# Turning chunks by VectorE blocks and a trip through DRAM in place of identity matmuls

## The chip, the cores and the metric

One core of a Trainium2 chip runs the whole kernel. The metric is the device time of one execution in microseconds (us); the median of the kernel before is 1278.88 us over three runs (1278.22 to 1279.74).

## What is computed

`x` is (8, 2048, 64) in fp32, `adj` a (2048, 2048) matrix A whose rows are a 0/1 pattern divided by the row's sum. Four layers, each `x = layernorm(x + f(x))` over the last 64:

```
layer 0:  out = sum over k of (T_k x) w_k[n] + b[n]    T_0 = I, T_1 = A, T_2 = 2 A A - I
          w_k[n] = sum over d < 16 of embedding[n, d] * weight[d, k]   (its own 64x64 per node n)
layer 1:  twice: z = relu((A z) W)
layer 2:  out = x Ws + (A x) Wn + bias
layer 3:  x1 = A x;  x2 = 2 A x1 - x;  out = [x, x1, x2, x1, x2] Wcat + bias
```

## The kernel before

**Layout.** The eight batches are four pairs, j = 0 to 3; a pair's 2 x 64 features are 128 columns. A pair's state lies in `nat` as [128 nodes, 16 node tiles x 128 features], and is handled in four chunks c of 512 columns. The 0/1 pattern of A stays in SBUF as `B` (128 x 16 x 2048, fp32r); the row factors are `rrep`.

**A pass.** One multiplication with A for one pair is a pass p. `split` (L743 on ScalarE, L874 on VectorE) writes the state as a high and a low fp32r part into `xs`. `mm` (L659, `pe_quarter` L605) multiplies: a chunk c of the result takes four quarters m of 8 matmuls of 128x512 each, 32 in all, into one PSUM bank. The state is the stationary operand, so the product comes out turned: features on partitions, nodes along the row. `scale` (L862) multiplies it by `rrep` into one slot per lane, `y = ring[:, 4 + n]` (n = j % 2), or for the first passes of pairs 0 and 1 into a slot of its own each.

Passes by number: 0 and 1 belong to layer 0, 2 and 3 to layer 1, 4 to layer 2, 5 and 6 to layer 3. After the product of chunk c comes `after`:
- p = 0: the scaled product is turned back to nodes on partitions by four identity matmuls (`pe_turned`, L618 to L621, called at L674), ScalarE copies it from PSUM into `nat` (L759); it is the source of pass 1. SyncE stores y itself into `y1d` (L1070) for later.
- p = 2, 3: y is weighed, `pe_weighed` (L623): four matmuls (each stands as two records in the profile) with y as stationary operand, which turns it on the way.
- p = 4, 5: the input of the chunk is needed too, turned. The step `ahead` does that with four identity matmuls on `nat` (L679) and a ScalarE copy into the lane's single slot `ring[:, n]` (L784); the weighing (L692) takes that slot and y, 8 matmuls, 16 records. For p = 5 y is also turned (L674) and copied into `stg` (L780), as source of pass 6.
- p = 6: y weighed, the last addition, the output.
Passes 3, 4 and 6 end in a layernorm: `centre`, `deviate`, `normed` (L902 to L922 on VectorE, L785 to L795 on ScalarE). GpSimd adds the biases (L1000).

**Order.** `order()` (L38) writes one list of steps by hand, and every engine runs its part of the list in order; semaphores tie them together. Each queue blocks on the first wait in it. `head()` loads A in tiles and runs pass 0 of pairs 0 and 1 as the tiles come; `second_pass0()` (L188) runs pass 1 of pair 0 while pair 1's pass-0 products are turned, then SyncE loads layer 0's weights (`weights0`, L1063). Then four stages, one per pair, run the per-node products of layer 0 (`T`, L717, each 10 matmuls of 128x512, with 8 VectorE accumulations at L974 per step) woven with quarters of the passes of the next pair (`weave`, L209). From `put("W")` (L284) on come two lanes: lane 0 is pair 2 and then pair 0, lane 1 pair 3 and then pair 1. They take turns; a lane's turn is one chunk, or one of the two `yield`s that stand before each pass and have no matmul of their own (the last chunk's `after` falls to the next turn as well). So now and then a lane runs two or three chunks with nothing of the other's between them.

**In a chunk of passes 4 and 5** the list reads: quarter 0 of chunk c, then `finish(c - 1)` (its `after`, and in pass 4 `deviate` of c-2, `centre` of c-1, `normed` of c-2), quarters 1 to 3, `ahead` of c, `scale` of c.

SyncE issues every DMA of the kernel in the order of the list. PSUM banks are handed out at L441 to L479; `xT_after` (L511) says when the slot `ring[:, n]` is free: when the weighing of the chunk before it is done.

Of the kernel before, what the change touches and what calls it, by code (L numbers as in the profile page):

```python
# [36 lines left out]

def order():  # L38
# [5 lines left out]
    def one_pass(j, p):  # L44

        norm = p in (3, 4, 6)

        def finish(c):
# [12 lines left out]
        for c, m in order:  # L61
            put("mm", j, p, c, m)
            if c > 0 and p >= 2 and m == (3 if c == 1 and order[2] == (1, 0) else 0):
                finish(c - 1)
            if m < 3:
                yield False
                continue
            if c > 0 and p < 2:
# [242 lines left out]
def gnn_stack(nc, xn, xt, at, rb, r16, emb, embt, b0, w01, w2, wbd, bias, eye, eps, out, zd, y1d, bd):  # L311
# [3 lines left out]
    with ctx:  # L315
# [47 lines left out]
        def way(general):  # L363
# [14 lines left out]
            s_wl = sem("wload")  # L378
# [3 lines left out]
            s_turn, s_turny, s_four, s_T = sem("turn"), sem("turny"), sem("four"), sem("T")  # L382
# [4 lines left out]
            s_lo, s_y, s_v = sem("lo"), sem("y"), sem("v")  # L387
            s_mean, s_var, s_norm, s_Lo, s_Sl = sem("mean"), sem("var"), sem("norm"), sem("Lo"), sem("Sl")
            s_acc, s_w0, s_twl, s_W = sem("acc"), sem("w0"), sem("twl"), sem("W")
            s_sum1, s_sum2, s_rec, s_Wc = sem("sum1"), sem("sum2"), sem("rec"), sem("Wc")  # L390
# [5 lines left out]
            else:  # L396
                s_at = [[sem(f"at{m}{c}") for c in range(PIECES.get(m, 1))] for m in range(NT)]
# [4 lines left out]

            def ahead(j, p, c):
                return Step("ahead", j, p, c)

            def after(j, p, c):
# [9 lines left out]
            turn_at = numbered("ahead")  # L416
            turny_at = {s: i + 1 for i, s in enumerate(s for s in STEPS if s.kind == "after" and s.p in (0, 5))}
            four_at = {s: i + 1 for i, s in enumerate(s for s in STEPS if s.kind == "after" and s.p > 1)}
            evict_at = {s: i + 1 for i, s in enumerate(
                s for s in STEPS if s.kind == "ahead" or s.kind == "after" and s.p in (0, 2, 5))}  # L420
# [18 lines left out]


# [4 lines left out]
            turn, held = [0, 1], {b: (s_evict, evict_at[after(1, 0, b)]) for b in range(2)}  # L445
# [14 lines left out]
            turn, held = [2, 3], {b: (s_evict, evict_at[after(1, 0, b)]) for b in (2, 3)}  # L460
# [7 lines left out]
            for i, s in enumerate(STEPS):  # L468
                if i == SECOND:
                    turn = turn + [6, 7]  # L470
                if s.kind == "after" and s.p == 0 and s.j < 2:
                    nbank_of[s, "turn"] = bank_of["prod", s.j, 0, s.c]
                    nbank_after[s, "turn"] = None
                elif s.kind == "ahead" or s.kind == "after" and s.p in (0, 5):
# [10 lines left out]
            held = [[(s_y1o[1], 64), (s_turny, turny_at[after(1, 0, c)])] for c in range(2)]  # L485
            for s in STEPS:
# [4 lines left out]
                elif s.kind == "scale" and s.p != 1:  # L491
                    y_after[s] = held[n]
                    if s.p == 0:
                        n_y1o[n] += 16
                        y1o_at[s.j, s.c] = n_y1o[n]
                        held[n] = [(s_y1o[n], n_y1o[n]), (s_turny, turny_at[after(s.j, 0, s.c)])]
                    else:
                        held[n] = [(s_four, four_at[after(s.j, s.p, s.c)])]
                if s.kind == "loadx":
# [14 lines left out]
            for s in STEPS:  # L514
                n = s.j % 2
                if s.kind == "ahead":
                    xT_after[s] = held_x[n]
                    held_x[n] = (s_four, four_at[after(s.j, s.p, s.c)])
                if s.kind == "centre" and s.p > 1:
                    if (s.j, s.p) == (2, 3):  # L520
                        sq_after[s] = (s_var, var_at[Step("deviate", 2, 3, s.c - 1)]) if s.c else None
                    else:
                        sq_after[s] = held_q[n]
                        held_q[n] = (s_var, var_at[Step("deviate", s.j, s.p, s.c)])

# [50 lines left out]

            def xs_free(j, p, c):
# [7 lines left out]
            def source_of(j, p, c):  # L585
# [8 lines left out]
                if p == 1:  # L594
                    return ch(nat[n], c), s_evict, evict_at[after(j, 0, c)]
# [4 lines left out]
                if p == 6:  # L600
                    return ch(stg[n], c), s_evict, evict_at[after(j, 5, c)]
# [28 lines left out]
            def pe_steps(pe, steps):  # L630
                for s in steps:
# [38 lines left out]
                    if s.kind == "after" and p in (0, 5):  # L670
# [4 lines left out]
                    if s.kind == "ahead":  # L675
                        pe.wait_ge(s_norm, norm_at[Step("normed", j, p - 1, c)])
                        if nbank_after[s, "turn"]:
                            pe.wait_ge(*nbank_after[s, "turn"])
                        pe_turned(pe, nbank_of[s, "turn"], ch(nat[n], c)).then_inc(s_turn, 1)  # L679
                    if s.kind == "after" and p > 1:  # L680
# [48 lines left out]
            def act_steps(ac, steps):  # L729
                for s in steps:  # L730
# [5 lines left out]
                    if s.kind == "tile" and not general:  # L736
                        cols = piece(k, c)
                        ac.wait_ge(s_at[k][c], 16)
# [4 lines left out]
                    if s.kind == "split":  # L743
                        src, landed, v = source_of(j, p, c)
                        ac.wait_ge(landed, v)
# [6 lines left out]
                    if s.kind == "after" and p == 0:  # L752
# [20 lines left out]
                    if s.kind == "after" and p == 5:  # L773
                        ac.wait_ge(s_turny, turny_at[s])
                        if j == 2:
                            ac.wait_ge(s_T, n_T)
                        else:
                            ac.wait_ge(s_hi, split_at[Step("split", j, 3, c)])
                            ac.wait_ge(s_lo, split_at[Step("split", j, 3, c)])
                        ac.copy(ch(stg[n], c), ps[:, nbank_of[s, "turn"], :]).then_inc(s_evict, 1)  # L780
                    if s.kind == "ahead":
                        ac.wait_ge(s_turn, turn_at[s])
                        ac.wait_ge(*xT_after[s])
                        ac.copy(ring[:, n, :], ps[:, nbank_of[s, "turn"], :]).then_inc(s_evict, 1)  # L784
# [52 lines left out]
            def dve_steps(dv, steps):  # L837
                for s in steps:
# [35 lines left out]
                    if s.kind == "split":  # L874
                        src, landed, value = source_of(j, p, c)
# [359 lines left out]
```

## Time and profile before

| | |
|---|---|
| median of 3 runs | 1278.88 us (1278.22 to 1279.74) |
| the profiled execution's own time | 1277.89 us |
| its span | 1276.1 us |
| TensorE matmul / weight load | 1249.3 us (98%) / 1046.2 us (82%) |
| VectorE | 730.8 us (57%) |
| ScalarE | 241.2 us (19%) |
| GpSimd | 62.2 us (5%) |
| DMA packets, bytes | 28517, 55.08 MB |

The profile's durations of single matmuls overlap (they are pipelined), so what one costs is read from the distance of the starts or from the chain of waits, which cuts the span into pieces that do not overlap. The chain covers the span from the last instruction backwards.

### The profile page before, as it was taken

How to read it: one execution, taken by the hardware profiler on the slowest of the kernel's cores; microseconds unless marked ns; L12 is line 12 of the kernel's file. 1: busy time of each engine (PE TensorE's matmuls, PEld its weight loads, DVE VectorE, ACT ScalarE, POOL GpSimd, SP SyncE). 2: the span in 40 equal slices, each digit the busy share in tenths (PEclk: the TensorE clock that was granted, in tenths of full speed). 3: DMA queues.
4: the chain of work that ended last, by engine and by line, in shares of the span. 5: the costliest groups of instructions: out<-in, count | busy, mean ns of one | idle time of the engine just before them, and what ended most of it. 6: DMA issues, size and time to landing. Idle time of an engine off the chain costs nothing.

```text
span 1276.1 us, 16492 instructions
## 1 busy us (share of the span) xinstructions
PE 1249.3 (98%) x6048; PEld 1046.2 (82%) x6048; DVE 730.8 (57%) x1819; ACT 241.2 (19%) x436; POOL 62.2 (5%) x52
## 2 busy tenths in 40 slices
PE   8999999999999999999999999999999999999996
PEld 6888888788878887878888888888888888888875
DVE  5836888786777777787624533551256245335424
ACT  5622111121112011110202121120202021211110
POOL 0000000000000000000001011000000010010000
PEclk9999999999999999999999999999999999999998
DMA  9732122221211111120000000010001000000000
GB/s 338 322 99 59 38 58 54 71 54 38 54 47 57 38 38 38 30 62 1 15 1 1 1 1 1 4 64 1 1 25 42 1 1 1 1 1 1 34 1 36
DMA packets 28517, 55.08 MB, mean 43 GB/s; under 512 B 3584, under 2 KB 14336, under 8 KB 26368
## 3 DMA queue, kind: packets, MB, share of 16 engines
q1 hardware_dynamic: 28432, 53.96, 12.9%
q8 instruction: 52, 0.85, 0.3%
q14 instruction: 33, 0.27, 0.1%
HBM read 41.89 MB, written 12.06 MB: 42 GB/s over the span
## 4 chain that ended last, share of the span: by engine, by line
PE 91%; DVE 5%; DMA 1%; issue 1%; ACT 1%; SPq 1%; DVEq 0%; ACTq 0%
PE ps L608 29%; PE ps L609 29%; PE ps L717 20%; PE ps L626 8%; PE ps L620 2%; PE ps L647 2%; PE ps L648 2%; DVE nat L974 1%; DVE ring L974 1%; DMA raw<-in_at 1%; DVE xs L884 1%; ACT xs L751 0%; SPq L1014 0%; DVE sml L916 0%; DVE sml L907 0%
## 5 line engine op out<-in xcount | busy, mean ns | idle before, releaser
L608 PE MATMUL ps<-B,xs 128*128 128x512 f32 x1664 | 658.1, 395 | 4.2 <-DVE xs L884 4.2
L609 PE MATMUL ps<-B,xs 128*128 128x512 f32 x1664 | 649.0, 390 | 0.0
L608 PEld LDWEIGHTS ps<-B,xs 128*128 128x128 f32 x1664 | 312.7, 188 | 67.8 <-ACT xs L751 3.9
L609 PEld LDWEIGHTS ps<-B,xs 128*128 128x128 f32 x1664 | 313.0, 188 | 61.7
L717 PE MATMUL ps<-Tw,xs 128*128 128x512 f32 x1280 | 309.4, 391 | 2.5 <-DVE ring L974 2.5
L717 PEld LDWEIGHTS ps<-Tw,xs 128*128 128x128 f32 x1280 | 238.6, 188 | 55.1 <-DVE ring L974 4.8
L872 DVE TENSOR_TENSOR ring<-ps,rrep 128x512 f32<-128x512 f32 x94 | 64.4, 689 | 277.6 <-PE ps L609 269.4
L974 DVE SCALAR_TENSOR_TENSOR nat<-ps,embn,nat 128x128 f32<-128x128 f32 x448 | 153.4, 342 | 51.0 <-PE ps L717 50.8
L974 DVE SCALAR_TENSOR_TENSOR ring<-ps,embn,ring 128x128 f32<-128x128 f32 x512 | 174.8, 341 | 0.0
L626 PEld LDWEIGHTS ps<-W,ring 128*128 128x128 f32 x896 | 110.4, 191 | 7.9 <-DVE ring L872 3.6
L626 PE MATMUL ps<-W,ring 128*128 128x128 f32 x896 | 113.2, 275 | 2.3 <-DVE ring L872 2.3
L789 ACT ACTIVATE ring<-nat 128x512 f32<-128x512 f32 x60 | 37.9, 632 | 313.2 <-DVE nat L911 313.2
L901 DVE TENSOR_TENSOR nat<-ps,nat 128x512 f32<-128x512 f32 x48 | 33.1, 690 | 66.7 <-PE ps L626 66.7
L1000 POOL TENSOR_TENSOR nat<-nat,bias 128x512 f32<-128x512 f32 x32 | 41.4, 1293 | 578.7 <-PE ps L620 578.7
L884 DVE TENSOR_TENSOR xs<-nat,xs 128x512 fp32r<-128x512 f32 x72 | 45.7, 685 | 21.3 <-ACT xs L751 20.9
L794 ACT ACTIVATE sml<-sml,epst 128x8 f32<-128x8 f32 x64 | 19.3, 301 | 186.8 <-DVE sml L916 186.8
L647 PE MATMUL ps<-B,xs 128*128 128x512 f32 x128 | 52.1, 407 | 2.4 <-DVE B L846 2.4
L784 ACT COPY ring<-ps 128x512 f32<-128x512 f32 x32 | 18.8, 587 | 177.6 <-PE ps L620 177.6
L648 PE MATMUL ps<-B,xs 128*128 128x512 f32 x128 | 51.4, 401 | 0.0
L993 POOL TENSOR_TENSOR nat<-nat,ring 128x512 f32<-128x512 f32 x16 | 20.6, 1289 | 586.9 <-DVE ring L974 586.9
L974 DVE SCALAR_TENSOR_TENSOR nat<-ps,embn,ring 128x128 f32<-128x128 f32 x64 | 22.3, 348 | 46.8 <-PE ps L717 46.0
L819 ACT CAST xs<-ring_x 128x512 fp32r<-128x512 f32 x32 | 19.6, 619 | 149.8 <-PE ps L717 116.7
(65 smaller groups left out, 625.9 us busy)
## 6 DMA issues: line engine op xcount, KB each, us to landing
raw<-in_at SPq DMA_DIRECT2D x13, 1024.0 KB, 17.0
ring<-in_xn SPq DMA_DIRECT2D x16, 256.0 KB, 2.9
ring_x<-in_xt SPq DMA_DIRECT2D x32, 128.0 KB, 3.3
ring_x<-y1d SPq DMA_DIRECT2D x32, 128.0 KB, 3.4
out<-nat SPq DMA_DIRECT2D x16, 256.0 KB, 2.4
y1d<-ring SPq DMA_DIRECT2D x14, 256.0 KB, 2.7
zd<-nat SPq DMA_DIRECT2D x12, 256.0 KB, 2.9
nat<-zd SPq DMA_DIRECT2D x3, 1024.0 KB, 4.9
```

Source lines behind the costliest of these rows:

```text
L608: pe.matmul(bank, x[:, 0, m, :], of, start=m == 0, stop=False)
L609: mm = pe.matmul(bank, x[:, 1, m, :], of, start=False, stop=ends and m == NT - 1)
L626: mm = pe.matmul(ps[:, bank, k * P:(k + 1) * P], src[:, k * P:(k + 1) * P], w, start=i == 0, stop=i == len(pairs) - 1)
L647: pe.matmul(bank, xs[n][:, 0, k, :], of, start=k == 0, stop=False)
L648: mm = pe.matmul(bank, xs[n][:, 1, k, :], of, start=False, stop=k == LAST)
L717: mm = pe.matmul(ps[:, 4 + 2 * p + q, :], src, Tw[:, wi, 512 * p:512 * p + 512], start=i == 0, stop=i == 4)
L789: ac.activation(square_slot(j, p, c), ch(nat[n], c), ACT.Square).then_inc(s_sq, 1)
L872: dv.tensor_tensor(to, ps[:, bank_of["prod", j, p, c], :], ch(rrep, 0 if general else c), ALU.mult).then_inc(s_y, 1)
L884: dv.tensor_tensor(lo, src, hi.bitcast(F32), ALU.subtract).then_inc(s_lo, 1)
L901: dv.tensor_tensor(v, bank, v, ALU.add).then_inc(s_v, 1)
L974: dv.scalar_tensor_tensor(sums[d % 2], ps[:, 4 + 2 * p:6 + 2 * p, i * C:(i + 1) * C], embn[:, t, d:d + 1], first[d] if d < 2 else sums[d % 2],
L1000: po.tensor_tensor(g, g, bias_t[:, p - 4, :].unsqueeze(1).to_broadcast([P, 8, C]), ALU.add).then_inc(s_pb, 1)
```

## The change

The four identity matmuls of a chunk and ScalarE's copy are replaced, for all chunks except those named by `on_pe`, by: VectorE transposes the 32x32 blocks of the chunk in place of the tile (`dv.transpose`, 128x512), SyncE stores the result (256 KB) into a DRAM scratch `td`, waits for it, and issues four loads of 64 KB, one for each group of 32 destination partitions, that bring the blocks to the place of the transposed chunk; each load reads runs of 32 elements (128 bytes). `ahead` is gone; its place is `turn` with k = 0, whose slot is still `ring[:, n]`. `turn` with k = 1 turns y into `nat` (p = 0) or `stg` (p = 5). In pass 0 `finish(c - 1)` moves up, from the end of chunk c to its quarter 1 (for c = 1 it stays at quarter 3). Six of the loads of A (tiles 9 to 14) share the semaphore of the tile seven earlier, and SyncE waits until ScalarE has read that tile. Some semaphores are merged. The store and the loads stand in SyncE's queue at the place of the step.

```diff
+def on_pe(j, p, c):
+    return p == 0 and (j == 0 or j > 1 and c == 3) or (j, p, c) == (1, 5, 3)
...
         def finish(c):
             put("after", j, p, c)
+            if p == 0 and not on_pe(j, p, c):
+                turn(c, 1)
...
         for c, m in order:
+            if p in (4, 5) and (c, m) == (0, 0):
+                turn(0, 0)
             put("mm", j, p, c, m)
+            if c > 0 and p == 0 and m == (3 if c == 1 else 1):
+                finish(c - 1)
             if c > 0 and p >= 2 and m == (3 if c == 1 and order[2] == (1, 0) else 0):
                 finish(c - 1)
+                if p in (4, 5):
+                    turn(c, 0)
...
-            if p in (4, 5):
-                put("ahead", j, p, c)
             put("scale", j, p, c)
+            if p == 5 and not on_pe(j, p, c):
+                turn(c, 1)
...
             if 2 <= i < 6:
                 put("after", 1, 0, i - 2)
+                put("turn", 1, 0, i - 2, 1)
+                put("back", 1, 0, i - 2, 1)
...
-                if s.kind == "ahead":
+                if s.kind == "turn" and s.k == 0:
                     xT_after[s] = held_x[n]
                     held_x[n] = (s_four, four_at[after(s.j, s.p, s.c)])
...
+            def turn_source(j, p, c, k):
+                return y_slot(j, p, c) if k else ch(nat[j % 2], c)
+
+            def turn_slot(j, p, c, k):
+                if k == 0:
+                    return ring[:, j % 2, :]
+                return ch(nat[j % 2] if p == 0 else stg[j % 2], c)
...
                         if p in (4, 5):
                             pe.wait_ge(s_W, 1)
-                            pe.wait_ge(s_evict, evict_at[ahead(j, p, c)])
+                            pe.wait_ge(*landed(j, p, c, 0))
...
+                    if s.kind == "turn":
+                        if k == 0:
+                            dv.wait_ge(s_norm, norm_at[Step("normed", j, p - 1, c)])
+                            dv.wait_ge(*xT_after[s])
+                        else:
+                            dv.wait_ge(s_y, scale_at[Step("scale", j, p, c)])
...
+                        dv.transpose(turn_slot(j, p, c, k), turn_source(j, p, c, k)).then_inc(s_turn, 1)
...
+                    if not s_at[m]:
+                        sp.wait_ge(s_nz, tile_at[Step("tile", 0, 0, 0, m - 7)])
...
+                    if s.kind == "turn":
+                        sp.wait_ge(s_turn, turn_at[s])
+                        sp.dma_start(td[n, k, c], turn_slot(j, p, c, k)).then_inc(s_away, 16)
+                    if s.kind == "back":
+                        v = moved_at[s._replace(kind="turn")]
+                        sp.wait_ge(s_away, 16 * turn_at[s._replace(kind="turn")])
+                        if v > 1:
+                            sp.wait_ge(s_back[n][k], 64 * (v - 1))
+
+                        blocks = td[n, k, c].rearrange("(a i) (t b m) -> b i t a m", i=32, t=4, m=32)
+                        for b in range(4):
+                            to = turn_slot(j, p, c, k)[32 * b:32 * b + 32, :].rearrange("i (t a m) -> i t a m", t=4, m=32)
+                            sp.dma_start(to, blocks[b]).then_inc(s_back[n][k], 16)
```

The helper `turn(c, k)` of `one_pass` puts the steps `turn` and `back` one after the other; `landed(j, p, c, k)` is the count of `s_back` at which a chunk's four loads have landed.

## Rows read from the trace of the kernel before

**Rows 1.** The page: busy time by engine, and the chain that ended last.
```profile
PE 1249.3 (98%) x6048; PEld 1046.2 (82%) x6048; DVE 730.8 (57%) x1819; ACT 241.2 (19%) x436; POOL 62.2 (5%) x52
...
PE 91%; DVE 5%; DMA 1%; issue 1%; ACT 1%; SPq 1%; DVEq 0%; ACTq 0%
```
**Rows 2.** Groups by shape, TensorE: count, busy us, mean ns, idle before.
```profile
L620 PE MATMUL ps<-identf,nat 128*128 128x128 f32 x128 | 19.1, 272 | 0.0
```
**Rows 3.** The chain in 1195 to 1235 us: start, us, what.
```profile
1198.29 0.23 PE ps L609
1198.53 0.44 PE ps L620 x4
```
**Rows 4.** The chain from 655 us: weighings of passes 4 and 5, pair 2.
```profile
664.02 1.78 PE ps L626 x16
...
674.44 1.78 PE ps L626 x16
...
683.98 1.78 PE ps L626 x16
...
698.96 1.78 PE ps L626 x16
...
735.23 1.79 PE ps L626 x16
...
746.12 1.79 PE ps L626 x16
...
756.13 1.79 PE ps L626 x16
```
**Rows 5.** DMA issues by line: count, KB each, median us from issue to landing.
```profile
y1d<-ring SPq DMA_DIRECT2D x14, 256.0 KB, 2.7
...
ring_x<-y1d SPq DMA_DIRECT2D x32, 128.0 KB, 3.4
...
ring<-in_w SPq DMA_DIRECT2D x2, 512.0 KB, 4.8
```
**Rows 6.** SyncE's queue in order of time: start, us, line, what.
```profile
81.48 4.65 SPq L1070 DMA_DIRECT2D y1d<-ring_x  x2
86.25 0.36 SPq L1066 DMA_DIRECT2D ring<-in_w  x1
...
110.62 0.61 SPq L1087 DMA_DIRECT2D ring_x<-in_xt  x1
111.28 0.60 SPq L1088 DMA_DIRECT2D ring_x<-y1d  x1
```
**Rows 7.** DMA in 153:155.05, 110.5:115, 79.6:81.35: packets, MB, share of 16 engines.
```profile
q1 hardware_dynamic: 144, 0.26, 33.1%
...
q1 hardware_dynamic: 288, 0.26, 20.1%
...
q1 hardware_dynamic: 144, 0.00, 4.4%
```
**Rows 8.** VectorE behind two weighings of pass 4, in order of time.
```profile
667.50 0.69 DVE L911 TENSOR_TENSOR nat<-nat,sml 128x512 f32<-128x512 f32 x1
...
679.22 0.69 DVE L921 TENSOR_TENSOR nat<-nat,sml 128x512 f32<-128x512 f32 x1
```
**Rows 9.** VectorE in 85 to 125 us, in order of time.
```profile
94.18 1.20 DVE L925 TENSOR_TENSOR ring<-ring 64x1024 f32<-64x1024 f32 x1
...
100.52 1.89 DVE L884 TENSOR_TENSOR xs<-nat,xs 128x512 fp32r<-128x512 f32 x3
...
107.71 0.69 DVE L872 TENSOR_TENSOR nat<-ps,rrep 128x512 f32<-128x512 f32 x1 [4.10 <-PE ps L609]
```
**Rows 10.** TensorE at the start, and stretch 12 to 13 us (busy, then clock).
```profile
14.05 0.63 PE L648 MATMUL ps<-B,xs 128*128 128x512 f32 x1
14.47 0.63 PE L647 MATMUL ps<-B,xs 128*128 128x512 f32 x1
...
12.00:13.00 1.00, 1.00 (x4) 0.81 (x3) 0.33 (x3) 0.67 (x2) 0.00 (x0) 1.00 1.01 365
```

More of the change, by code:

```diff
@@ L396, in way @@
             else:
-                s_at = [[sem(f"at{m}{c}") for c in range(PIECES.get(m, 1))] for m in range(NT)]
+                s_at = [[sem(f"at{m}{c}") for c in range(PIECES.get(m, 1))] if m < 9 or m == LAST else None
+                        for m in range(NT)]
                 s_r = [sem(f"r{c}") for c in range(NC)]
@@ L438, in way, with turned, landed @@
                     held[i] = s
+            def turned(j, p, c):
+                if on_pe(j, p, c):
+                    return s_turny, turny_at[after(j, p, c)]
+                return s_turn, turn_at[Step("turn", j, p, c, 1)]
+            def landed(j, p, c, k):
+                return s_back[j % 2][k], 64 * moved_at[Step("turn", j, p, c, k)]
             bank_of = {("prod", j, 0, c): 4 - 4 * j + c for j in range(2) for c in range(NC)}
             bank_after = {}
-            turn, held = [0, 1], {b: (s_evict, evict_at[after(1, 0, b)]) for b in range(2)}
+            turn, held = [0, 1], {b: (s_y, scale_at[Step("scale", 1, 0, b)]) for b in range(2)}
             for i, s in enumerate(STEPS):
@@ L459, in way @@
             nbank_of, nbank_after = {}, {}
-            turn, held = [2, 3], {b: (s_evict, evict_at[after(1, 0, b)]) for b in (2, 3)}
+            turn, held = [2, 3], {b: (s_y, scale_at[Step("scale", 1, 0, b)]) for b in (2, 3)}
             def take(use, frees):
@@ L484, in way @@
             y1o_at = {}
-            held = [[(s_y1o[1], 64), (s_turny, turny_at[after(1, 0, c)])] for c in range(2)]
+            held = [[(s_y1o[1], 64), turned(1, 0, c)] for c in range(2)]
             for s in STEPS:
@@ L594, in source_of @@
                 if p == 1:
-                    return ch(nat[n], c), s_evict, evict_at[after(j, 0, c)]
+                    return ch(nat[n], c), *((s_evict, evict_at[after(j, 0, c)]) if on_pe(j, 0, c) else landed(j, 0, c, 1))
                 if p == 2 and j < 2:
@@ L669, in pe_steps @@
                             mm.then_inc(s_prod, 1)
-                    if s.kind == "after" and p in (0, 5):
+                    if s.kind == "after" and on_pe(j, p, c):
                         pe.wait_ge(s_y, scale_at[Step("scale", j, p, c)])
@@ L751, in act_steps @@
                             ac.copy(part_of(j, 0, c), src).then_inc(s_hi, 1)
-                    if s.kind == "after" and p == 0:
+                    if s.kind == "after" and p == 0 and on_pe(j, p, c):
                         ac.wait_ge(s_turny, turny_at[s])
@@ L772, in act_steps @@
                         ac.copy(ch(to, c), ps[:, nbank_of[s, "four"], :]).then_inc(s_evict, 1)
-                    if s.kind == "after" and p == 5:
+                    if s.kind == "after" and p == 5 and on_pe(j, p, c):
                         ac.wait_ge(s_turny, turny_at[s])
[L775 to L779, printed above, removed]
+                        ac.wait_ge(s_hi, split_at[Step("split", j, 3, c)])
+                        ac.wait_ge(s_lo, split_at[Step("split", j, 3, c)])
                         ac.copy(ch(stg[n], c), ps[:, nbank_of[s, "turn"], :]).then_inc(s_evict, 1)
[L781 to L784, printed above, removed]
                     if s.kind == "centre":
```

82 lines of the change are left out of this document (47 added, 35 removed).

## The prediction

> **What bounds the kernel now.** I read the page first. TensorE is busy in 98% of the span and holds 91% of the chain that ended last [rows 1], so whatever leaves its queue comes off the time, and whatever makes it wait goes on it. Next the turns by identity matmul: 256 of them, four to a chunk of 128x512, 64 chunks; the largest of their three groups is [rows 2], the others have 120 and 8. The mean of one, 272 ns, is not its price: the chain of waits gives four of them 0.44 us between their neighbours, as it gives 0.23 us to one product matmul [rows 3]. Then I read the end stage, from 613 us, where two pairs of batches ("lanes") take turns by chunk. The 16-matmul pieces of the chain are the weighings of passes 4 and 5, 32 chunks. Their starts show how long TensorE has other work between one weighing and the next of the same lane: 15 us when the other lane has a chunk there, but 9.5 to 10.9 us when it has none [rows 4]. Last, VectorE's rows behind a weighing, the DMA rows, and the stretch from 80 to 113 us.
>
> **Part 1: what leaves TensorE.** By `on_pe`, 4 chunks of pair 0 and the last chunks of pairs 2 and 3 in pass 0, and one of pass 5, stay: 7. The 57 others go: 32 "ahead", 15 of pass 5, 10 of pass 0. 57 x 0.44 = 25.1 us off the path [rows 3]. The Trainium skill ("TensorE: Matmul & The Clock Gate", section "Part 4: PE-mode transpose") gives some 275 ns for one turn inside a kernel; by that 228 of them would be 63 us and the sum below would end near 1273. The trace agrees with 275 as a duration (272), not as a price, so that end gets no chance of its own.
>
> **Part 2: what VectorE and ScalarE get.** 57 transposes of 128x512. No such row exists; the nearest, one 128x512 operation, takes 0.69 [rows 9], and I take that; bounds 0.35 (twice as fast) and 1.3. That is 39 us on an engine that is busy 57%. ScalarE loses 57 evictions, which were off the path and are worth nothing. The added load matters only through the waits of part 4.
>
> **Part 3: the new way of a chunk (R).** Transpose, store to DRAM, wait for its landing on SyncE's queue, four loads. The store: 2.7 us to landing as y1d's (2.3 to 2.9 over all stores of this size) [rows 5]. Each load is 64 KB in 512 runs of 128 bytes. Issues of loads with rearranged patterns start 0.66 apart [rows 6] and land in 3.4 [rows 5]; the fourth lands 3 x 0.66 + 3.4 = 5.4 after the first is issued. Do the short runs take longer than that? From the share of 16 engines, windows of 2.05, 4.5 and 1.75 us: 2 KB runs 84 ns, 1 KB runs 56 ns, 4-byte runs 8.6 ns each [rows 7]. A line through the first two gives 31 ns at 128 bytes, one through the last two 14; an engine has 128 runs in the four loads, so 1.8 to 4.0 us, inside the 5.4. I take 5.5. R = 0.69 + 2.7 + 5.5 + 0.3 for the hand-overs = 9.2 us. Low end: 0.35 + 2.3 + 0.2 + (3 x 0.45 + 2.9) = 7.1. High end: runs that cost what 1 KB does, 128 x 0.056 = 7.2, plus 1.8 of issue and confirmation = 9.0 for the loads, R = 12.6 to 13.
>
> **Part 4: who waits (47 of the 57 are in the end stage).** The turned input lies in one slot per lane (`ring[:, n]`). So the turn of chunk c waits for the weighing of c-1 (`xT_after`), and TensorE, in order, waits at the weighing of c (`landed`). Between the two it has the distance of their starts [rows 4], less the weighing (1.78) and the turns that are gone (0.44 in pass 4, 0.88 in pass 5): 10.42 gives 8.2 and 9.54 gives 7.3 in pass 4; 10.89 gives 8.2 and 10.01 gives 7.3 in pass 5. Against that stands VectorE's work queued ahead of the turn, plus R. In pass 4 the centring of c-1 comes first: for c = 1 from the group's end at 665.80 to 668.19, 2.4 us; for c = 2 to the end of the norm at 679.91 after a group that ended at 676.22, 3.7 us [rows 4, 8]. In pass 5 only the addition, 0.75. So:
> - Pass 4, c = 1: 2.4 + 9.2 = 11.6, against 8.2 twice and 7.3 twice: 2 x 3.4 + 2 x 4.3 = 15.4.
> - Pass 4, c = 2: 12.9 against 7.3, twice (pairs 2 and 0): 11.2.
> - Pass 5: 9.95 against 8.2 twice, 7.3 five times: 3.5 + 13.3; and the last chunk of pair 1, where only 24 matmuls (5.45) stand between: 4.5. Together 21.3.
> That is 14 waits, 47.9 us. Elsewhere the cover is 10.4 us or more (12.8 for c = 3 of pass 4, against 12.9) and I cost it at nothing; it goes if R is over 10. The products of pass 5 (k = 1) have 16 to 60 us until their splits; their loads hold SyncE's queue some 5.5 us, which hits the next turn by 1.7 at most, and then the wait before it has already moved it: nothing.
>
> **Part 5: the head of the kernel.** Pair 1's four turns stand in SyncE's queue ahead of `weights0`. Each holds it for a y1d store's issue, the landing and four issues: 0.45 + 2.7 + 0.1 + 2.6 = 5.85 us. From about 82 us, near the y1d stores that start at 81.48, the weights would be asked for at 104.7 instead of 86.25 and land 4.8 later, at 109.6 [rows 5, 6]; VectorE's work on them starts there instead of at 94.18, a shift of 15.4 [rows 9]. Behind it in VectorE's queue stand pair 1's splits (now at 100.52) that TensorE wants at 107.5, when pair 0's pass ends and its last scaling starts [rows 9]. Slack of about 6.3, minus a handful of tenths for the hand-over: TensorE waits 9.3 us. With 4.7 a turn the shift is 11 and the wait 4.7. In passes 0 of pairs 2 and 3 the turn has about 10 us until its split; 1 us for both together, as SyncE's queue also holds the fetches. The raw loads that now wait for the tile seven earlier are costed at nothing: the six loads between are still in flight then and hide it; without them the head would wait for each load's landing.
>
> **Sum.** 47.9 + 9.3 + 1 - 25.1 = +33. The profiled execution took 1277.9 (1.0 under the median of 1278.88, a difference I ignore): 1311.
>
> **The rivals.**
> - *All lands in time (faster).* R under 6.4 us hides every wait but the head's: 1277.9 - 25.1 + 4.7 = 1257. For it: landings of 2.3 and 2.9 exist. Against: those two alone with three more issues and the transpose are 7.1. 8%.
> - *Break-even.* All at the low end, R = 7.1: pass 4 2 x 1.3 + 2 x 2.2 + 2 x 3.5 = 14.0, pass 5 5.2, head 4.7, minus 25.1: 1277. 13%, a third of it on either side of the 0.2%.
> - *The waits also cost clock.* In the first microseconds product matmuls start 0.42 to 0.43 apart, about what the lower of the two levels (1.2 GHz) would make of the 0.23 later, though the granted clock is given as 1.00 there [rows 3, 10]. If each of the eight waits over 3.4 us cost a stretch like the 14 matmuls that go at this pace, 14 x 0.2 = 2.8 us, that is 22 more: 1333. Against it: nothing shows what a wait of 4 us does here. 11%.
> - *Short runs are slow.* At R = 12.6: pass 4 47 for c = 1 and 2 and 13 for the rest, pass 5 48, head 23, weave 1, minus 25: 1385. The Trainium skill ("DMA: Bandwidth & Descriptors", section "Rules for kernel authors") says to turn data by the DMA's own transpose and not by a plain copy with a rearranged pattern, which it puts at 19 times slower. By it this rival would be the likely one. Here VectorE does the fine part, and the small runs of [rows 7] show no such price. 10%.
>
> **How the numbers follow.** My forecast, 58%, spans 1285 to 1345 for R from 7.8 to 10.2. The range 1270 to 1350 leaves out the full gain and the slow runs. Under 0.2% (2.6 us, about what a measurement can tell) 5%; faster 12%; slower 83%.
>
> **What would show it.** Identity matmuls x28; TensorE waits at L626's successor put down to the DMA that reads `td`, 13 or 14 of them, 2 to 6 us each, in pairs; loads landing 3.4 after issue; VectorE busy near 770; the weights asked for near 105 and the first per-node product near 122 instead of 113. It is wrong if a weighing follows its predecessor by 9.1 us with no wait, or if waits appear where the cover is 15 us.

## The result, and the profile after

The changed kernel takes 1340.12 us (median of 4 runs, 1338.52 to 1345.48); the kernel before took 1278.55 beside it (1277.48 to 1279.74). The ratio is 1.0489 with a 95% interval of 1.0457 to 1.0520: slower by 61.6 us, where the prediction said slower by 33, range 1270 to 1350. The profiled execution took 1338.52 (span 1336.7, mean granted clock 0.975, before 0.996).

The page of the changed kernel: busy time by engine, DMA packets, and the chain that ended last, by engine.

```profile
PE 1247.7 (93%) x5820; PEld 1039.0 (78%) x5820; DVE 766.3 (57%) x1876; ACT 209.0 (16%) x379; POOL 62.3 (5%) x52
...
DMA packets 157111, 84.99 MB, mean 64 GB/s; under 512 B 124880, under 2 KB 135632, under 8 KB 154960
...
PE 68%; DVE 11%; DMA 11%; SPq 6%; issue 3%; ACT 1%; DVEq 0%; ACTq 0%
```

Beside [rows 1]: TensorE runs 228 matmuls fewer and holds 68% of the chain instead of 91%. What came in is DMA (11%) and SyncE's queue (6%), the trip that a turned chunk now makes. The chain shows how often that trip was the last thing missing.

The page, DMA issues by line (count, KB each, median us from issue to landing):

```profile
td<-ring SPq DMA_DIRECT2D x32, 256.0 KB, 2.0
ring<-td SPq DMA_DIRECT2D x128, 64.0 KB, 2.5
```

The store of a turned input lands in 2.0 (that of a product of pass 5 in 2.4) and a load in runs of 128 bytes in 2.5, against 2.7 for y1d's store and 3.4 for y1d's loads [rows 5]. Who waits, on TensorE (us in total, times, longest):

```profile
PE ps L671 <- DMA ring<-td: 40.5, 15, 4.9
PE ps L653 <- DVE xs L917: 19.2, 6, 12.8
PE ps L665 <- DVE ring L905: 6.4, 3, 3.0
```

L671 is the weighing (L626 before), L653 the product (L608 before), L665 the identity matmul that stayed. 15 weighings wait for the loads of their turned input; one product waits 12.8 us, in the head.

**Where the 60.6 us of the two profiled spans lie.** The per-node products T cut the kernel into three. First and last start of the 1280 of them, by source line, before and after:

```profile
L717 PE MATMUL ps<-Tw,xs x1280: 387/389/502, 112.9 to 604.0; 128*128 128x512 f32 x183
```

```profile
L757 PE MATMUL ps<-Tw,xs x1280: 387/389/628, 126.7 to 624.3; 128*128 128x512 f32 x183
```

The head got longer by 13.8 us, the woven middle by 6.5 (491.1 to 497.6), the end stage by 40.3 (672.1 to 712.4). To each, add the turns that it lost, at 0.44 [rows 3]: 4, 6 and 47 chunks, 1.8, 2.6 and 20.7 us. So the new costs are 15.6, 9.1 and 61.0, the gain is 25.1, and the rest is +60.6.

**One trip in the end stage**, pair 2, pass 4. SyncE's queue, VectorE's and TensorE's in 688 to 712 us (start, us, what, idle before and its releaser):

```profile
689.30 0.33 SPq L1123 DMA_DIRECT2D td<-ring  x1
691.28 2.60 SPq L1133 DMA_DIRECT2D ring<-td  x4
702.34 0.33 SPq L1123 DMA_DIRECT2D td<-ring  x1
704.48 2.78 SPq L1133 DMA_DIRECT2D ring<-td  x4
```

```profile
688.57 0.70 DVE L932 STREAM_TRANSPOSE ring<-nat 128x512 f32<-128x512 f32 x1
...
701.61 0.70 DVE L932 STREAM_TRANSPOSE ring<-nat 128x512 f32<-128x512 f32 x1
```

```profile
695.98 2.02 PE L671 MATMUL ps<-W,ring 128*128 128x128 f32 x16 [1.54 <-DMA ring<-td]
709.36 3.06 PE L671 MATMUL ps<-W,ring 128*128 128x128 f32 x16 [4.05 <-DMA ring<-td]
```

From the start of the transpose to the weighing: 7.4 us and 7.75 us. That is R, forecast at 9.2. Although R is shorter, the second weighing waits 4.05; and it then takes 3.06 us where the first took 2.02. The clock says why (stretch, TensorE busy, granted clock, DMA share, GB/s):

```profile
709.00:710.00 1.00, 0.64 (x6) 1.00 0.00 0
710.00:711.00 1.00, 1.00 (x8) 0.56 0.00 0
711.00:713.00 2.00, 2.00 (x9) 0.50 0.00 0
713.00:714.00 1.00, 1.00 (x5) 0.73 0.00 0
714.00:716.00 2.00, 2.00 (x10) 1.00 0.00 0
```

The clock is still at its upper level (2.4 GHz) for the first part of a microsecond after the wait, then at the lower (1.2 GHz), and back at 714. Work lost: 0.44 + 2 x 0.50 + 0.27 = 1.7 us, paid after the wait ended and put down to no wait at all.

Such a spell of lower clock follows eight of the fifteen waits for turned inputs, each costing 1.7 us, the last (1286 to 1294) 3.4. It is not the length of a wait alone that decides. In the same form, from the ends of waits of 4.41, 2.26, 3.74 and 3.06 us on:

```profile
894.00:899.00 5.00, 4.92 (x23) 0.66 0.28 48
1187.00:1192.00 5.00, 4.75 (x22) 0.66 0.00 0
1080.60:1086.00 5.40, 5.39 (x32) 1.00 0.00 0
1175.60:1181.00 5.40, 5.33 (x32) 1.00 0.00 0
```

Read in stretches of 1 us, TensorE's busy time times the missing share of the clock adds up to 14.5 us in the end stage, 5.1 in the middle (three spells) and 3.5 in the head (two spells). In the kernel before it is nothing in all three.

### The profile page after: what moved, and what is told of

Its sections match the earlier page's. It is cut to its first block, busy times and chain, and to the rows that moved or that the text cites. A ratio compares the mean times of both kernels' runs of the same rounds, so it can differ in the third digit from the quotient of the medians.

```text
span 1336.7 us, 16321 instructions
## 1 busy us (share of the span) xinstructions
PE 1247.7 (93%) x5820; PEld 1039.0 (78%) x5820; DVE 766.3 (57%) x1876; ACT 209.0 (16%) x379; POOL 62.3 (5%) x52
## 4 chain that ended last, share of the span: by engine, by line
PE 68%; DVE 11%; DMA 11%; SPq 6%; issue 3%; ACT 1%; DVEq 0%; ACTq 0%
PE ps L653 21%; PE ps L654 21%; PE ps L757 16%; PE ps L671 7%; SPq L1133 5%; DMA td<-ring 3%; DMA ring<-td 3%; PE ps L692 2%; PE ps L693 2%; DVE nat L1022 2%; DVE ring L1022 2%; DMA td<-nat 1%; DMA ring_x<-y1d 1%; DVE sml L955 1%; DVE ring L905 1%
## 5 line engine op out<-in xcount | busy, mean ns | idle before, releaser
L653 PE MATMUL ps<-B,xs 128*128 128x512 f32 x1664 | 660.3, 397 | 19.2 <-DVE xs L917 19.2
L653 PEld LDWEIGHTS ps<-B,xs 128*128 128x128 f32 x1664 | 316.2, 190 | 85.3 <-issue 17.6
L757 PEld LDWEIGHTS ps<-Tw,xs 128*128 128x128 f32 x1280 | 242.0, 190 | 54.9 <-DVE ring L1022 4.7
L671 PE MATMUL ps<-W,ring 128*128 128x128 f32 x896 | 123.4, 290 | 43.5 <-DMA ring<-td 40.5
L671 PEld LDWEIGHTS ps<-W,ring 128*128 128x128 f32 x896 | 118.6, 203 | 56.5 <-issue 47.7
L791 ACT CAST xs<-nat 128x512 fp32r<-128x512 f32 x72 | 39.7, 615 | 37.7 <-DMA nat<-zd 24.6
## 6 DMA issues: line engine op xcount, KB each, us to landing
raw<-in_at SPq DMA_DIRECT2D x13, 1024.0 KB, 16.7
```

What stands on the lines that cost most here:

```text
L653: pe.matmul(bank, x[:, 0, m, :], of, start=m == 0, stop=False)
L671: mm = pe.matmul(ps[:, bank, k * P:(k + 1) * P], src[:, k * P:(k + 1) * P], w, start=i == 0, stop=i == len(pairs) - 1)
L757: mm = pe.matmul(ps[:, 4 + 2 * p + q, :], src, Tw[:, wi, 512 * p:512 * p + 512], start=i == 0, stop=i == 4)
L791: ac.copy(part_of(j, 0, c), src).then_inc(s_hi, 1)
```

## The experiments

My theory after the result, called A: the loss is the sum of single causes, each at its place: the waits for turned inputs in the end stage, the clock that they cost, and SyncE's queue in the head and the middle. The rivals differ by experiment. All kernels are edits of the changed one (1340.12) unless said otherwise. The kernel before took 1277.9 to 1278.4 us beside each group.

**1. The 32 inputs back on TensorE.** The step `ahead` returns as before; the 15 products of pass 5 and pass 0 stay on the new way.

```diff
-            if p in (4, 5) and (c, m) == (0, 0):
-                turn(0, 0)
...
-                if p in (4, 5):
-                    turn(c, 0)
...
+            if p in (4, 5):
+                put("ahead", j, p, c)
             put("scale", j, p, c)
...
```

> The turned input of passes 4 and 5 (32 chunks) goes back to four identity matmuls and a ScalarE copy; the 15 products of pass 5 and the 10 of pass 0 keep the new way. Theory A (the end stage loses 61 us by the wait for the single slot per lane and by the lower clock after the longest of these waits): those 61 us go and the 32 x 0.44 = 14 us gained come back, 1340 - 61 + 14 = 1293. Theory B (the new transfers and VectorE's transposes slow everything in proportion to their number): 32/57 of the 61.6 us go, 1305.

Measured: 1296.47 (1292.07 to 1297.60), ratio 1.0132 (1.0108 to 1.0156). Its end stage takes 670.7 us (623.4 to 1294.1). Less the 15 turns that are still gone there (6.6), the stage of the kernel before would be 665.5, so 5.2 us of the 61.0 are left. With the inputs' trips gone, 55.8 of them are gone; the products' trips of pass 5 alone cost next to nothing.

**2. Pass 0 back on TensorE** (pairs 1, 2 and 3, 10 chunks), **and 3. pair 1's four alone.**

```diff
-    return p == 0 and (j == 0 or j > 1 and c == 3) or (j, p, c) == (1, 5, 3)
+    return p == 0 and (j == 0 or j in (1, 2, 3) or j > 1 and c == 3) or (j, p, c) == (1, 5, 3)
```

For pair 1 alone the inner list is `(1,)`; with all three, `finish(c - 1)` of pass 0 stands at the end of chunk c again.

> The 10 chunks of pass 0 (pair 1's four, three each of pairs 2 and 3) go back to TensorE, with the order of before there; passes 4 and 5 keep the new way. Theory A (SyncE's queue is held by store, landing and loads, so that layer 0's weights come 20 us late and the fetches of the per-node stages late too: 15.5 us at the head and 9.2 in the stages after, by the distance of marks in the two traces): 1340 - 24.7 + 4.4 = 1320. Theory B (in proportion to the number): 10/57 of 61.6 us, 1329.

> Edit: only pair 1's four pass-0 chunks are turned by TensorE again (head of the kernel); pairs 2 and 3 keep the new way. Theory A (the head loses by the place of the weights behind the four turns in SyncE's queue, and no later slack takes that up): the first per-node product starts again near 113 instead of 126.7, and the time falls by that 13.8 us: 1326. Of the 22 us that came back with all ten pass-0 chunks on TensorE, some 8 would then belong to pairs 2 and 3. Theory B (part of the head's loss is absorbed later, since the passes woven into the per-node products wait for their fetches anyway): less than half of it, 1333 to 1336, and most of the 22 us would be pairs 2 and 3.

Measured: 1317.81 (1311.06 to 1319.91), ratio 1.0288 (1.0259 to 1.0318), and 1328.30 (1326.04 to 1331.16), ratio 1.0399 (1.0383 to 1.0415). Pair 1's four chunks are worth 11.8 us, the six of pairs 2 and 3 another 10.5 by the medians, 6.4 by the middle stages of the two profiles (499.0 and 492.6). With all ten back the first T starts at 112.2 and 40.0 us of waits for turned inputs are left: the head and the end stage do not touch each other. Both times lie nearest to theory A.

**4. Filled waits.** Before 14 weighings TensorE multiplies something that is overwritten afterwards. The counts in the edit add up to 115 matmuls of 128x512, and the trace shows 115; the 121 and 27.5 us of the expectation are a wrong sum (115 x 0.23 = 26.5).

```diff
+                            for _ in range(FILL.get((j, p, c), 0) if not general else 0):
+                                pe.matmul(ps[:, bank, :], B[:, 0, 0:P], B[:, 0, 0:512], start=True, stop=True)
                             pe.wait_ge(*landed(j, p, c, 0))
...
```

> Nothing is undone: ahead of the weighings that waited for the four loads, TensorE gets 5 to 12 extra matmuls of 128x512 into the bank that the weighing overwrites, each 0.23 us, fewer than fit into the wait that the trace shows there (14 places, 121 matmuls, 27.5 us in all), so that it is not idle for over 2 us. Theory A (part of the loss is the clock, which is granted at 0.50 for 3.4 us after a long wait, some 9 times in the end stage at 1.7 us each): 1340 - 12 to 15, 1327. If the clock costs nothing: 1340, or up to 5 us more where a filler is longer than its wait.

Measured: 1328.04 (1324.33 to 1333.37), ratio 1.0384 (1.0348 to 1.0420): 12 us faster by doing more work (8.1 by the spans of the two profiled executions). Its end stage, from the last T at 623.4 to 1328.6, takes 705.2 us against 712.4. Its weighings that wait:

```profile
PE ps L673 <- DMA ring<-td: 16.7, 10, 3.7
```

All waits of the stage fell from 47.2 (40.5 + 6.7 others) to 21.4 (16.7 + 4.7 others). With the fillers that is 21.4 + 26.5 = 47.9 us, no less than the 47.2 that they stand in for, and the stage is 7.2 shorter all the same: 7.9 us to explain. The granted clock explains 6.6 of them: the loss counted as above is 7.9 us where the changed kernel has 14.5, and the spells left follow the three longest waits that are left (3.1 to 3.7 us). The fill was not complete. Three of the 14 places (24 matmuls) had no wait in the changed kernel, and three of its waits (4.41, 4.30 and 3.06) got no filler.

**5. Two slots per lane for the turned input**, the turn issued one chunk earlier.

```diff
             if p in (4, 5) and (c, m) == (0, 0):
                 turn(0, 0)
+                turn(1, 0)
...
-                if p in (4, 5):
-                    turn(c, 0)
+                if p in (4, 5) and c < 3:
+                    turn(c + 1, 0)
...
+                if k == 0 and c % 2:
+                    return W[:, 5:9, :].rearrange("p a b -> p (a b)") if j % 2 else part_slot(0)
...
```

> The turned input gets a second slot per lane (the old ring_g for one lane, the free end of a longer W for the other), and each chunk is turned one chunk earlier, so that 15 us of TensorE's work lie between its transpose and its weighing. The number of transposes, stores and loads is the same. Theory A (the chain through the single slot costs 40.5 us of waits and the clock about 15): 1340 - 55 = 1285, no wait of L671's successor for the loads from td. Theory B (the transfers as such): 1335 to 1340. Between them: if SyncE's queue, which both lanes share, becomes the bound, half the waits stay, 1312.

Measured: 1305.40 (1304.42 to 1306.03), ratio 1.0208 (1.0191 to 1.0225): 34.7 us faster, but 20 short of A's 1285. TensorE's waits in its end stage:

```profile
PE ps L657 <- DVE xs L921: 14.2, 2, 12.8
PE ps L675 <- DMA ring<-td: 7.4, 4, 3.3
```

The single slot was the cause of the waits for turned inputs: 40.5 became 7.4 + 1.7. In their place one of 12.8 us appeared. The chain in 838 to 886 us shows what it is (start, us, what):

```profile
854.88 2.15 DMA td<-ring
...
859.69 2.61 DMA td<-W
...
864.97 2.65 DMA td<-stg
...
870.88 0.62 SPq L1189
...
873.00 3.29 DMA td<-ring
...
878.97 2.56 DMA td<-stg
...
884.32 5.18 DMA nat<-zd
```

The reload of pair 0's state stands behind five trips and the outputs (L1189) in SyncE's queue, each trip a landing and four issues.

**6. Layer 0's weights asked for first**, ahead of pair 1's turns.

```diff
                 put("after", 1, 0, i - 2)
+                if i == 2:
+                    put("wload")
                 put("turn", 1, 0, i - 2, 1)
...
-                    if s.kind == "weights0":
+                    if s.kind == "wload":
```

> Only the place of two DMA issues changes in SyncE's list: layer 0's weights are asked for ahead of pair 1's four turns instead of behind them. Theory A (at the head TensorE waits for what stands in VectorE's queue behind these weights, 12.8 us, and the clock falls with it): 1340 - 13 to 15 = 1326, the first per-node product near 112 us instead of 126.7. Rival (pair 1's turned products themselves come too late, since the four turns still hold SyncE's queue to 107 us): the wait moves to them, 1335 to 1340.

Measured: 1330.61 (1328.94 to 1331.89), ratio 1.0407 (1.0390 to 1.0425), between the two. The first T starts at 114.6 instead of 126.7, but part of it comes back in the middle: the last T starts at 618.2 instead of 624.3, so 6.1 of the 12.1 are left at that point. The trace shows where the other 6.0 went: in the middle the identity matmuls wait 8.4 us instead of 5.6, and the clock costs 8.6 instead of 5.1. By the medians 9.5 us came back of the head's 11.8 (experiment 3).

**7. Two slots and pass 0 on TensorE**, and **8. that with the outputs of pairs 2, 3, 0 and the two late reloads issued by ScalarE's queue**; **9. two slots and the moved outputs, pass 0 as in the change.**

```diff
-                    if s.kind == "reload":
+                    if s.kind == "reload" and j == 2:
...
-                    if s.kind == "out":
+                    if s.kind == "out" and j == 1:
...
+                    if s.kind == "reload" and j != 2:
+                        for i in range(NC):
+                            ac.wait_ge(s_z[n][i], 16)
+                        ac.wait_ge(s_out[n], 64)
+                        ac.dma_start(nat[n][:], zd[j]).then_inc(s_re[n], 16)
+                    if s.kind == "out" and j != 1:
+                        ac.wait_ge(s_norm, norm_at[Step("normed", j, 6, c)])
+                        ac.dma_start(out[j, :, cols], ch(nat[n], c)).then_inc(s_out[n], 16)
```

> Both of the earlier edits together: the second slot per lane, and pass 0 back on TensorE. If the losses are separate, 1305.4 - 22.3 = 1283. If they hide each other (the end stage only starts earlier and waits for the same thing), above 1290; the wait of 12.8 us for pair 0's splits stays in either case.

> As the one before, and the outputs of pairs 2, 3 and 0 and the reloads of pairs 0 and 1 are issued from ScalarE's queue, no longer from SyncE's. Theory A (the 12.8 us wait with two slots is pair 0's reload, asked for at 884 us behind four turns in SyncE's queue, and the clock that falls with it): 1283 - 13 to 17 = 1268, faster than the kernel before by 10. Rival (the reload itself, or the traffic, takes that long): 1283.

> Two slots per lane and outputs and reloads from ScalarE's queue, pass 0 as in the change. Theory A: 1305.4 - 15 = 1290; what is left over the kernel before is then the head and the per-node stages (24.7 less their gain of 4.4). Rival as in the run before: 1305.

Measured, in this order: 1285.93 (1281.76 to 1289.16), ratio 1.0066 (1.0043 to 1.0089); **1271.37 (1268.80 to 1274.06), ratio 0.9950 (0.9935 to 0.9966)**; 1294.01 (1290.64 to 1298.18), ratio 1.0134 (1.0106 to 1.0162). The reload's wait, 13.0 us in the first of them, is gone in the second. The second beats the kernel before by 0.5%. Its waits for turned inputs on TensorE:

```profile
PE ps L671 <- DMA ring<-td: 6.6, 3, 3.6
...
PE ps L671 <- DMA W<-td: 1.7, 1, 1.7
```

Its end stage takes 664.6 us (603.3 to 1267.9): 672.1 of before, less 20.7 of turns, plus 9.0 more of waits than before (12.4 against 3.4), makes 660.4. The remaining 4.2 have a place in the granted clock: three spells, which cost 4.9 us while TensorE was busy. So the price of 0.44 for a turn holds within a microsecond over 47 turns.

**10. A control on the kernel before**: only the moved outputs and reloads.

> A control, made on the kernel before: the outputs of pairs 2, 3 and 0 and the two late reloads are issued by ScalarE's queue instead of SyncE's, as in the version of the changed kernel that came out 0.5% faster than the kernel before. If that gain comes from the turns that left TensorE: no change here, 1278 (1276 to 1280), since TensorE waits in the kernel before for nothing that stands behind an output in SyncE's queue. Rival: the moved outputs would have made any version faster, 1270 or less, and the turns would not be what gained.

Measured: 1277.69 (11 runs, 1277.18 to 1279.97) against 1278.10 (15 runs), ratio 0.9998 (0.9989 to 1.0007). The moved outputs give nothing where no turns crowd SyncE's queue, so the gain of experiment 8 over the kernel before comes with the turns that left TensorE.

**11. The store made twice, one landing after the other.**

```diff
                         sp.dma_start(td[n, k, c], turn_slot(j, p, c, k)).then_inc(s_away, 16)
+                        sp.wait_ge(s_away, 32 * turn_at[s] - 16)
+                        sp.dma_start(td[n, k, c], turn_slot(j, p, c, k)).then_inc(s_away, 16)
...
```

> Edit: SyncE stores each turned chunk twice, one after the other, and waits for the landing in between, so that the way of a chunk is longer by one landing (2.0 us in the profile of the changed kernel) and 0.3 us. Nothing else changes. Theory A (the waits at the weighings are cover minus this way): 13 waits of the end stage grow by 2.3 each, 30 us; the third chunks of pass 4, just covered until now, begin to wait, 4 us; the head gets four times 2.3, 9 us; the weave 4; and longer waits take a further 5 to 10 us of clock. 1340 + 30 + 4 + 9 + 4 + 8 = 1395. Theory B (the waits are set by something that the way of the chunk only shares, such as VectorE's place in the order): less than half of it, under 1365.

Measured: 1426.60 (1421.74 to 1432.32), ratio 1.1161 (1.1130 to 1.1192), 86.5 us more than the change, and above both theories. Its waits:

```profile
PE ps L671 <- DMA ring<-td: 85.5, 20, 9.1
PE ps L653 <- DVE xs L917: 30.0, 6, 21.8
```

The head's wait grew by 9.0 (12.8 to 21.8), as said for four landings. The waits for turned inputs grew by 45.0 where 34 were expected. That fits a queue in which the next trip starts later too, so that an added landing is paid more than once. Its end stage takes 780.0 us; less 672.1, plus 20.7, less 85.5 and 4.5 of other added waits, 38.6 us are left. The clock is 36.6 of them, counted as above (mean of the whole execution 0.947).

**12. In pass 5 the product's trip behind the next input's.** Why this one: only part of the 40.5 us follows from the length of a trip. Which pass a wait belongs to follows from its place in the list of steps. An example, two weighings of the changed kernel:

```profile
797.23 1.95 PE L671 MATMUL ps<-W,ring 128*128 128x128 f32 x16
805.30 3.39 PE L671 MATMUL ps<-W,ring 128*128 128x128 f32 x16 [4.30 <-DMA ring<-td]
```

In the list the first weighing of pair 3's pass 4 stands one quarter behind the last of pair 2's pass 5. So 797.23 is that last one, and the wait of 4.30 us belongs to pass 4; so does the one of 3.06 (pair 1, behind pair 0). By this order 23.2 us (8 waits) are in pass 4 and 17.3 (7 waits) in pass 5. The expectation below says 26.9 in pass 5; that counts three waits of pass 4 (4.30, 3.06 and 2.26) to it. With R = 7.5 the covers of the prediction leave 16.4 us at the second and third chunks of pass 4, where 15.8 were measured. They leave nothing at the first chunks, where 7.4 were measured, and 7.7 in pass 5, where 17.3 were. Some 16 us are thus not the trip's own length. SyncE's queue of the changed kernel in 786 to 800 us:

```profile
786.04 0.41 SPq L1123 DMA_DIRECT2D td<-ring  x1
790.27 2.60 SPq L1133 DMA_DIRECT2D ring<-td  x4
792.91 0.62 SPq L1123 DMA_DIRECT2D td<-stg  x1
795.42 2.60 SPq L1133 DMA_DIRECT2D stg<-td  x4
798.06 0.62 SPq L1123 DMA_DIRECT2D td<-ring  x1
```

```profile
791.54 0.67 DVE L932 STREAM_TRANSPOSE ring<-nat 128x512 f32<-128x512 f32 x1
```

Two things happen to an input here. The store issued at 786.04, right behind the four loads of a product (783.19 to 785.79), landed after 4.2 us instead of 2.0. And the input transposed by 792.2, that of the weighing at 805.30, is stored only at 798.06, 5.9 us later, because the trip of the other lane's product stands ahead of it.

```diff
                 if p in (4, 5):
                     turn(c, 0)
+                if p == 5:
+                    turn(c - 1, 1)
...
-            if p == 5 and not on_pe(j, p, c):
+            if p == 5 and c == 3 and not on_pe(j, p, c):
                 turn(c, 1)
```

> Edit: in pass 5 the product of chunk c is turned (transpose, store, four loads) directly after the next chunk's input instead of directly after its own scaling, so that the lane's next input no longer finds that trip ahead of it in SyncE's queue. In the profile of the changed kernel 26.9 of the 40.5 us of waits on turned inputs are in pass 5, where the cover less a way of 7.5 us would leave 7.7. Theory A (the rest is SyncE's queue: an input's store stands up to 6 us behind the product's trip, or lands in 4.2 instead of 2.0 us next to its loads): the waits fall by some 15 us and with them 3 to 5 us of clock: 1321. Theory B (the trips only change places, and now hold up the other lane's inputs): the waits fall by less than half of that, 1332 or more. Theory C (the order in VectorE's queue makes the waits): no change, 1340.

Measured: 1341.86 (1340.92 to 1346.72), ratio 1.0504 (1.0479 to 1.0529): no change against the 1340.12. The waits for turned inputs, in total and the largest, and SyncE's queue ahead of it:

```profile
PE ps L673 <- DMA ring<-td: 43.4, 15, 9.7
```

```profile
813.88 3.76 PE L673 MATMUL ps<-W,ring 128*128 128x128 f32 x16 [9.67 <-DMA ring<-td]
```

```profile
795.97 0.62 SPq L1125 DMA_DIRECT2D td<-stg  x1
798.63 2.60 SPq L1135 DMA_DIRECT2D stg<-td  x4
801.27 0.62 SPq L1125 DMA_DIRECT2D td<-stg  x1
804.00 2.60 SPq L1135 DMA_DIRECT2D stg<-td  x4
806.64 0.62 SPq L1125 DMA_DIRECT2D td<-ring  x1
```

By total it is theory C's number, but by mechanism B's. The waits of pass 5 shrank from 17.3 us to 12.0 (4.87 to 2.19, 4.41 to 2.78, 2.38 to 1.70). Those of pass 4 grew from 23.2 to 31.4; the two first chunks alone grew by more, from 4.30 to 9.67 and from 3.06 to 8.22. These are inputs of the other lane. That of the first was transposed by 795.4, and its store at 806.64 comes after two product trips. Thus SyncE's queue sets these waits; another order in the same queue only moves them.

## Why the prediction was right, and where it was not

The sign and its mechanism held: TensorE gives up 25 us and then stands at the weighings and in the head for longer than that. The time of 1340 lies inside the range and inside the forecast's own 1285 to 1345, but 29 us above its centre. That it lies inside is in part luck: R came out at 7.4 to 7.75, below the 7.8 to 10.2 that the forecast stood for. With R = 7.5 the prediction's own covers leave 24.1 us in the end stage instead of 47.9, and its sum ends at 1287. The long R stood in for SyncE's queue and the clock. Its sum against the profiled spans:

| term | forecast | measured |
|---|---|---|
| 57 turns leave TensorE | -25.1 | -25.1 (price checked in experiment 8 within a microsecond) |
| waits in the end stage | +47.9 | +43.8 (40.5 for inputs, 3.3 others) |
| clock in the end stage | 0 | +17.2 (what is left of 61.0; 14.5 of it counted) |
| head | +9.3 (waits of TensorE) | +15.6 |
| middle | +1 | +9.1 |
| sum | +33 | +60.6 |

- **Part 2** held: a transpose of 128x512 takes 0.70 (taken: 0.69), VectorE is busy 766 (said: near 770).
- **Part 3** was too dear: R is 7.4 to 7.75, not 9.2. The landings were taken from y1d's rows (2.7 and 3.4) and are 2.0 and 2.5. Why they are shorter was not tried. That the short runs hide inside the issues held: from the first load's issue (691.28) to the weighing (695.98) it is 4.7 us, against 5.5 taken. The Trainium skill ("DMA: Bandwidth & Descriptors", section "Rules for kernel authors") warns of a plain copy with a rearranged pattern, 19 times slower than a DMA transpose. No DMA transpose ran here, so no ratio is shown, and VectorE did the fine part of the turn. What the trace shows is that the plain copy of the 32x32 blocks in runs of 128 bytes costs 2.5 us a load.
- **Part 4**: the covers held where a lane follows itself in pass 4 (second and third chunks): 26.6 forecast, 15.8 measured, from the smaller R, for which they give 16.4. The first chunks of pass 4 of pairs 3 and 1 were forecast at nothing ("Elsewhere the cover is 10.4 us or more") and wait 7.4; from the start of the transpose at 791.54 to where the weighing would have started there are only 9.5. Pass 5: 21.3 forecast, 17.3 measured, though R alone would give 7.7. The step that failed is "their loads hold SyncE's queue some 5.5 us, which hits the next turn by 1.7 at most, and then the wait before it has already moved it: nothing". The queue did hold inputs up, by 5.9 us in the example, and experiment 12 shows that it decides these waits. The two errors (R too long, the queue at nothing) nearly cancelled in the total of the waits, so 47.9 against 40.5 is no proof of the term.
- **The rival of the clock** had 11% and was no rival but part of what happened. "Nothing shows what a wait of 4 us does here" was true of the trace before; the run of the change shows it. Priced at 8 x 2.8 = 22 us, it came to 14.5 in the end stage and 23.1 in the whole kernel, counted from the granted clock. It should have stood in the sum with a half of its price at least. The Trainium skill ("TensorE: Matmul & The Clock Gate", section "HAM oscillation — how this bites in real kernels") says that matmuls after a wait for a DMA run at the lower rate and puts the price at half of the time at that rate. The trace agrees on the price: 1.7 us lost in the stretch of 709 to 714, at a granted clock of 0.50 to 0.56 for most of it. It differs in that the first part of a microsecond after the wait still ran at the upper level, and that waits of 3.74 and 3.06 us were followed by no drop.
- **Part 5**: the place was right, the size not. The weights were asked for at 107.16 (said: 104.7), and VectorE's work on them starts at 112.32 (said: 109.6), because a turn holds the queue 6.5 us (81.27 to 107.16, four of them) and not 5.85. TensorE waits 12.8 instead of 9.3; in 119.5 to 126.7 the mean granted clock is 0.76, a cost of 1.7 not in the sum. Another spell of 1.7 at 24 to 28 us stands in this profile and in that of experiment 12 but in none of the other ten edits, so it is hardly the change's.
- **The middle**, "1 us for both together, as SyncE's queue also holds the fetches": 9.1. Experiments 2 and 3 put 6.4 to 10.5 us on the six chunks of pairs 2 and 3. The fetches of the per-node products stand behind the trips. SyncE's queue after:

```profile
260.79 0.33 SPq L1123 DMA_DIRECT2D td<-nat  x1
262.77 2.61 SPq L1133 DMA_DIRECT2D nat<-td  x4
265.49 0.64 SPq L1150 DMA_DIRECT2D ring_x<-in_xt  x1
```

  The traces account for the 9.1. TensorE's waits in the middle grew by 4.9 (5.9 to 10.8): two waits of the identity matmuls that stayed, 3.04 and 2.60, are new, and two short ones (0.37 each) are gone. The clock adds 5.1, in three spells of which two follow these two waits. Together that is 10.0.
- **A rival's condition** was misread: "R under 6.4 us hides every wait but the head's". By the prediction's own covers the third chunks of pass 4 need R under 3.6 and the last of pass 5 under 4.7; at R = 6.4 there would still be 11.5 us of waits, so 1257 belongs to an R under 3.6.
- **The signs named**: 28 identity matmuls as said, 15 waits (said: 13 or 14) of 0.3 to 4.9 us (said: 2 to 6), the weights asked for at 107 (said: near 105); the first T came at 126.7 and not near 122. Loads landing after 3.4 was wrong. One sign of being wrong showed, in its smallest form: a wait of 0.27 us at a weighing that stood 17.3 us behind its predecessor before (pair 3, pass 5, third chunk).

What stays open: 14.5 of the 17.2 us of clock in the end stage are counted. The other 2.7 may lie in how a wait is read, from the modelled end of the last matmul (0.39 long) and not from where the next would have started (0.23 later): 15 x 0.16 = 2.4 us, an estimate. Which wait is followed by a drop is open too: those of 2.14, 2.26, 2.48, 2.65 and of 4.05 and more were, those of 2.38, 3.06 and 3.74 were not, nor those under 2.

## What to carry to other kernels

When work leaves the bound engine for a trip through DRAM, the trip's length is not all that counts: how many slots it has and what else stands in its queue decide with it. One more slot and other queues for the outputs turned 61 us of loss, with pass 0 left on TensorE, into a gain of 6.5. Count for every step on a DMA queue the time that it holds the queue (landing plus issues, 5 to 6.5 us here) and list everything behind it. And where a change makes TensorE wait some microseconds, put the clock in the sum beside the wait (here 1.7 us behind about every second wait).

## What the runs showed of the hardware

- A wait of 4.05 us cost 1.7 us more afterwards, at a granted clock of 0.50 that set in less than a microsecond after work had resumed. One of 2.26 us cost as much, those of 3.74 and 3.06 us nothing. 115 added matmuls before the weighings made the kernel 12 us faster.
- A VectorE transpose in 32x32 blocks of 128x512 fp32 takes 0.70 us, as much as an addition of that size.
- 64 KB loads in runs of 128 bytes landed in 2.5 us, less than y1d's 128 KB loads (3.4 before, [rows 5]).
- A 256 KB store issued just behind four such loads landed in 4.2 us instead of 2.0 (one case, at 786.04; why was not tried).
- Outputs issued by ScalarE's queue instead of SyncE's gained 14.6 us where turns crowded SyncE's queue (experiments 7 and 8) and nothing where they did not (experiment 10). The Trainium skill ("DMA: Bandwidth & Descriptors", section "Rules for kernel authors") says that spreading DMAs over engines saves only issue time; here what it saved was a wait of 13 us for a reload's place in the queue.
